# Layer norms' normalising, a convolution tap and copies moved from VectorE to ScalarE in a fused decoder layer

## The chip, the cores and the metric

One core of a Trainium2 chip runs the whole kernel. The metric is device time of one execution in microseconds, median of the runs made.

## The reference

The input x has 16 sequences of 128 positions and 256 features. Three sub-layers are added to it, each behind a layer norm without gain:

```python
x = x + mamba(layernorm(x))             # in_proj, 4-tap convolution, silu, scan of 16 states, gate, out_proj
x = x + mlstm(layernorm(x), ctx, ctx)   # 4 heads of 64; gates from concat(q, k, v) @ kernel
x = x + ffn(layernorm(x))               # 6 attention nodes in a graph, then a layer norm with gain and offset
```

Where it matters here: the convolution is `sum over k of w[k] * x[t + k - 1] + b`. The gates take `concat([q, k, v]) @ kernel` with k = v = ctx. The mLSTM's head is divided by `normalizer + 1e-6` and then normalised over its 64 features, `(h - mean) * rsqrt(var + 1e-6) * scale`. The silu is computed with a tanh, so weights of the convolution are halved ahead (`convh`).

## The kernel before

The batch is cut into 8 groups of 2 sequences (256 columns, or 128 partitions by 2 by 256 features). Each group goes through three streams of steps, and all engines walk one list, `ORDER`, in which the steps of neighbouring groups are interleaved: each engine runs, of each step, what it has to do in it, in order. `ORDER` is sorted by numbers written out by hand for each step (`A_AT`, `U_AT`, `X_AT`, `P_AT`), counted in steps of the feed-forward net of the group that runs at that time. The streams are:

- **A**, eleven steps (`mamba_in`): norm 1 (step 0), its transposes (1), four input projections (2 to 5) through one PSUM bank `MA`, the convolution on VectorE (4), silu and gate, the projections of step sizes; then **U**, 32 *units* (`unit`): on ScalarE two exponentials for the decay (`dec`, L753, two buffers), on VectorE a product to feed (L972), a scan (L979) and a weighing (L990), on TensorE the sums over states (L487), and after eight units a `gather`.
- **X**, the mLSTM (`mlstm`, `head_scores`, `head_values`, `head_norm`, `mlstm_out`): out projection and norm 2 (`ml` 1), gates, four heads, their norm, norm 3 (`out` 0) and its transposes (`out` 1), which give node -1 of the net.
- **F**, the net (`queries`, `keys`, `values`, `node_max`, `node_score`, `node_attend`, `node_edge`, `node_out`) with 6 nodes one after the other, and `ffn_out` with norm 4, gain, offset, the residual and the store.
- **P**, the preparation of the net's weights, only at the start.

While F of group g runs, the units of group g+1 end, its X runs and the units of group g+2 begin. F of the last group runs alone.

A layer norm (`layer_norm` on VectorE) is BATCH_NORM_STATS (L911), aggregation (L915), the addition of epsilon (L917), then a wait for ScalarE (`rstd_of`: a logarithm L678 and an exponential L679) and two TENSOR_SCALAR (L920), one per sequence:

```python
for b in range(GB):
    last = v.tensor_scalar(dst[:, b, :], src(b), mean_var[:, b, 0:1], inv[:, b:b + 1],
                           ALU.subtract, ALU.mult)
```

The convolution reads `hs_pad`, which ScalarE copies from `MA` (L705); its first tap is a TENSOR_SCALAR (L934), the three others are L941. `head_values` copies each head out of PSUM (L1049). `head_norm` divides all heads by their denominators (L1062), takes the mean (L1063), subtracts it (L1065), squares (L1066), sums (L1067) and scales (L1070, L1073). The gate product (L516) multiplies three times two blocks of `wgate`.

## Time and profile before

| | us |
|---|---|
| median of 3 runs | 1309.74 (1309.69 to 1315.06) |
| the profiled execution | 1308.01 |
| its span, first to last instruction | 1306.2 |
| VectorE (DVE) busy | 1053.6 |
| TensorE (PE) busy | 1098.0 |
| ScalarE (ACT) busy | 720.6 |

The rows come from the profiled execution. A row of the waits gives the time for which an engine stood idle and the engine, tile and line that released it; a row of the groups gives busy time (overlap counted once) and the mean duration of one; a row of the timeline gives start, duration, engine, line, and in brackets the idle time before it. PE is TensorE's matmul, PEld its weight load. Busy time of stretches is cut where the net of a group ends (L655).

### The profile page before, as it was taken

How to read it: one execution, taken by the hardware profiler on the slowest of the kernel's cores; microseconds unless marked ns; L12 is line 12 of the kernel's file. 1: busy time of each engine (PE TensorE's matmuls, PEld its weight loads, DVE VectorE, ACT ScalarE, POOL GpSimd, SP SyncE). 2: the span in 40 equal slices, each digit the busy share in tenths (PEclk: the TensorE clock that was granted, in tenths of full speed). 3: DMA queues.
4: the chain of work that ended last, by engine and by line, in shares of the span. 5: the costliest groups of instructions: out<-in, count | busy, mean ns of one | idle time of the engine just before them, and what ended most of it. 6: DMA issues, size and time to landing. Idle time of an engine off the chain costs nothing. (4 is left out here: it accounts for less than half of the span.)

```text
span 1306.2 us, 27811 instructions
## 1 busy us (share of the span) xinstructions
PE 1098.0 (84%) x11504; PEld 822.0 (63%) x11504; DVE 1053.6 (81%) x1683; ACT 720.6 (55%) x1692; POOL 2.9 (0%) x10
## 2 busy tenths in 40 slices
PE   3845668988999899989988998899888988897886
PEld 2723445766676667666666666666666666676665
DVE  2289887799999999999999999999999889725112
ACT  1434532576657665776567556755576646444332
POOL 0000000000000000000000000000000000000000
PEclk9767775999999999999999999999999989999998
DMA  6440343004100410030112211030104000000000
GB/s 190 122 178 32 107 153 113 33 3 130 41 26 33 132 42 25 34 105 28 50 49 62 71 50 49 16 117 33 58 3 130 33 25 34 2 1 10 2 1 9
DMA packets 53710, 76.14 MB, mean 58 GB/s; under 512 B 15376, under 2 KB 38672, under 8 KB 53456
## 3 DMA queue, kind: packets, MB, share of 16 engines
q1 hardware_dynamic: 53584, 74.37, 17.9%
q8 instruction: 90, 1.47, 0.5%
q14 instruction: 36, 0.29, 0.1%
HBM read 63.60 MB, written 10.75 MB: 57 GB/s over the span
## 5 line engine op out<-in xcount | busy, mean ns | idle before, releaser
L979 DVE TENSOR_TENSOR_SCAN unit_buf<-dec,unit_buf 128x512 f32<-128x512 f32 x256 | 311.9, 1218 | 11.7 <-ACT dec L753 11.0
L753 ACT ACTIVATE dec<-dts,a_neg 128x254 f32<-128x254 f32 x512 | 225.6, 499 | 42.5 <-DVE unit_buf L979 37.3
L972 DVE TENSOR_TENSOR unit_buf<-dtus,bs 128x512 f32<-128x512 f32 x256 | 175.0, 686 | 6.3 <-DMA dtus<-dt_rows 2.5
L990 DVE TENSOR_TENSOR unit_buf<-unit_buf,cs 128x512 f32<-128x512 f32 x256 | 175.3, 685 | 0.5
L1087 DVE TENSOR_REDUCE mx<-heads 128x16 f32<-128x2048 f32 x48 | 109.2, 2276 | 50.1 <-PE heads L602 50.0
L487 PE MATMUL ps<-unit_buf,fold 128*32 128x256 f32 x1024 | 89.0, 420 | 52.4 <-DVE unit_buf L990 52.3
L825 ACT ACTIVATE pr<-heads 128x512 f32<-128x512 f32 x192 | 99.1, 603 | 49.0 <-PE heads L617 49.0
L571 PE MATMUL ps<-node,wq_f 128*128 128x256 f32 x384 | 93.6, 387 | 7.8 <-ACT node L840 7.8
L640 PE MATMUL heads<-node,we_f 128*128 128x256 f32 x384 | 94.7, 389 | 0.0
L647 PE MATMUL heads<-aT,wo_f 128*128 128x256 f32 x384 | 93.7, 387 | 0.9 <-DVE aT L1096 0.9
L581 PE MATMUL heads<-wv_f,node 128*128 128x256 f32 x384 | 91.8, 382 | 0.0
L571 PEld LDWEIGHTS ps<-node,wq_f 128*128 128x128 f32 x384 | 70.6, 190 | 27.8 <-ACT node L840 11.1
L647 PEld LDWEIGHTS heads<-aT,wo_f 128*128 128x128 f32 x384 | 69.6, 190 | 18.7 <-issue 5.8
L640 PEld LDWEIGHTS heads<-node,we_f 128*128 128x128 f32 x384 | 69.5, 190 | 17.7 <-issue 9.9
L556 PE MATMUL ps<-node,wk_f 128*128 128x256 f32 x320 | 80.0, 393 | 0.0
L581 PEld LDWEIGHTS heads<-wv_f,node 128*128 128x128 f32 x384 | 71.8, 190 | 12.1 <-issue 2.9
L815 ACT ACTIVATE kT<-ps,fb 128x256 f32<-128x256 f32 x80 | 33.4, 469 | 79.4 <-PE ps L556 79.4
L487 PEld LDWEIGHTS ps<-unit_buf,fold 128*32 128x32 f32 x1024 | 21.9, 111 | 86.8 <-DVE unit_buf L990 54.2
L602 PE MATMUL heads<-kT,qT 32*128 32x128 f32 x1536 | 57.2, 285 | 20.8 <-issue 11.7
L452 PE MATMUL ps<-th,win 128*128 128x256 f32 x256 | 71.5, 427 | 3.6 <-ACT hs_pad L705 1.5
L602 PEld LDWEIGHTS heads<-kT,qT 32*128 32x128 f32 x1536 | 48.9, 188 | 37.1 <-issue 36.3
L840 ACT ACTIVATE node<-heads,fb 128x256 f32<-128x256 f32 x96 | 40.1, 468 | 56.1 <-PE heads L647 56.0
(178 smaller groups left out, 1777.8 us busy)
## 6 DMA issues: line engine op xcount, KB each, us to landing
dts<-dt_rows SPq DMA_DIRECT2D x32, 512.0 KB, 3.8
dtus<-dt_rows SPq DMA_DIRECT2D x32, 512.0 KB, 5.2
node<-in_w_edgeT SPq DMA_DIRECT2D x18, 256.0 KB, 3.6
dt_rows<-dt SPq DMA_DIRECT2D x32, 128.0 KB, 2.4
dt_rows<-th SPq DMA_DIRECT2D x32, 128.0 KB, 2.5
bs<-bc_rows SPq DMA_DIRECT2D x32, 128.0 KB, 4.6
cs<-bc_rows SPq DMA_DIRECT2D x32, 128.0 KB, 4.3
xin<-in_x SPq DMA_DIRECT2D x8, 256.0 KB, 6.2
```

The costliest lines, as they stand in the source:

```text
L487: last = mm(MY[r0:r0 + SD, 0:T], fold[:], prd[(i * UNITS + k) % PRDS][:, a, :], start=(q == 0), stop=(q == NGRP - 1), tile_position=(0, r0))
L571: last = mm(FA[:, a * T:(a + 1) * T], wq_f[c][:, k, a * P:(a + 1) * P], src[:, k, :], start=(a == 0 and k == 0), stop=(k == HC - 1), skip_ ...
L581: last = mm(X3[:, b * H:(b + 1) * H], node[SLOT[GRAPH[c]["v"]]][:, k, b * L:(b + 1) * L], wv_f[c][:, k, :], start=(k == 0), stop=(k == HC ...
L602: last = mm(heads[:, h, to], qT[at], kT[c % 2][at], start=True, stop=True, tile_position=(FD * h, 0))
L640: mm(X1[:, a * T:(a + 1) * T], we_f[c][:, k, a * P:(a + 1) * P], src[:, k, :], start=(a == 0 and k == 0), stop=False, skip_group_check=True)
L647: last = mm(X1[:, a * T:(a + 1) * T], wo_f[c][:, k, a * P:(a + 1) * P], aT[:, k, :], start=False, stop=(k == HC - 1), skip_group_check=True)
L753: last = fn(dec[k % 2][:, a, :, 1:L], dts[c % 2][:, blk, :].rearrange("p (b t) -> p b t", b=GB)[:, :, 1:L], ACT.Exp, scale=a_neg[:, c, blk ...
L825: fn(pr[s][:], heads[:, :, s * L:(s + 1) * L], ACT.Exp, scale=FD ** -0.5).then_inc(sig["prob"], 1)
L972: v.tensor_tensor(inf[k % 2][:], dtus[c % 2][:, 2 * pair:2 * pair + 2, :], bs[:, q:q + 1, :].broadcast_to([P, 2, T]), ALU.mult).then_inc(s ...
L979: v.tensor_tensor_scan(hst[k % 2][:].rearrange("p a b -> p (a b)"), dec[k % 2][:].rearrange("p a b t -> p (a b t)"), inf[k % 2][:].rearran ...
L990: v.tensor_tensor(prd[(i * UNITS + k) % PRDS][:], hst[k % 2][:], cs[:, q:q + 1, :].broadcast_to([P, 2, T]), ALU.mult).then_inc(sig["outflo ...
L1087: v.tensor_reduce(mx[:].rearrange("p (h s) -> p h s", h=HPC)[:, :, 0:STEPS], heads[:].rearrange("p h (s k) -> p h s k", s=STEPS), AX.X, AL ...
```

## The change

Normalising moves to ScalarE in all four norms: `layer_norm` on VectorE ends with a negation of the mean and the addition of epsilon, and `normalise` on ScalarE multiplies the negated mean by the root and applies both as scale and bias of an Identity. VectorE waits before it overwrites mean and variance the next time, and in norm 4 for the rows. The tap with k = 1 of the convolution, which needs no shift, is taken by ScalarE straight from PSUM with the bias; VectorE does the taps 0, 2 and 3. `head_values` moves to ScalarE. In `head_norm` the heads are not divided by the denominator any more: mean and variance are taken of the undivided heads, the variance is multiplied twice by the reciprocal denominator before epsilon is added, the root once after; the square is done by ScalarE, between two waits. The two blocks of gate kernel rows for k and v are added once, and the gate product has four blocks instead of six. All four tables of numbers are others.

```diff
-    ln_var1=1, ln_rstd1=1, hvar=1, hrstd=1,
+    ln_var1=1, ln_rstd1=1, hcentre=1, hsquare=1, hvar=1, hrstd=1,
...
-A_AT = [-90, -86, -76, -69, -62, -58, -57, -52, -44, -43, -42]
+A_AT = [-99, -84, -76, -71, -69, -58, -57, -52, -50, -47, -40]
...
-X_AT = [18, 38, 43, 44, 47, 48, 49, 51, 53, 54, 55, 57, 58, 60, 63, 65]
+X_AT = [4, 38, 43, 44, 48, 49, 50, 52, 54, 55, 56, 57, 58, 59, 63, 65]
...
 # TensorE, mlstm step 3
-                    for k in range(3 * HC):
+                    for k in range(2 * HC):
...
 # ScalarE
+            def normalise(chain, n, i, src, mean_var, inv, dst):
+                rstd_of(chain, f"ln_var{n}", f"ln_rstd{n}", i, inv[:])
+                after(act, f"ln_rstd{n}", i, 1)
+                for b in range(GB):
+                    m = chain.mark(fn(mean_var[:, b, 0:1], mean_var[:, b, 0:1], ACT.Copy, scale=inv[:, b:b + 1]))
+                chain.wait(m)
+                for b in range(GB):
+                    last = fn(dst[:, b, :], src(b), ACT.Identity, scale=inv[:, b:b + 1], bias=mean_var[:, b, 0:1])
+                return last
...
+                    after(act, "y_ready", i - 2, IC)
+                    for a in range(2):
+                        c = 2 * j + a
+                        last = fn(u[p][:, c, :], MA[:, a * T:(a + 1) * T], ACT.Identity,
+                                  scale=convh[:, 5 + c * 4:6 + c * 4], bias=convh[:, c:c + 1])
                     last.then_inc(sig["inproj_read"], 1)
...
+            def head_values(i, h):
+                after(act, "h_ps", i, h + 1)
+                fn(hrow[:, :, h, :], MB[:, 0:GB * XP].rearrange("p (b d) -> p b d", b=GB), ACT.Copy
+                   ).then_inc(sig["h_read"], 1)
+
             def head_norm(i, _):
+                after(act, "hcentre", i, 1)
+                fn(hsq, hn, ACT.Square).then_inc(sig["hsquare"], 1)
                 rstd_of(m_chain, "hvar", "hrstd", i, hva[:])
...
 # VectorE, layer_norm
+                v.tensor_scalar(mean_var[:, :, 0], mean_var[:, :, 0], -1.0, None, ALU.mult)
                 v.tensor_scalar(inv[:], mean_var[:, :, 1], eps, None, ALU.add).then_inc(sig[f"ln_var{n}"], 1)
-                after(dve, f"ln_rstd{n}", i, 1)
-                for b in range(GB):
-                    last = v.tensor_scalar(dst[:, b, :], src(b), mean_var[:, b, 0:1], inv[:, b:b + 1],
-                                           ALU.subtract, ALU.mult)
-                return last
...
 # VectorE, convolution
-                    for k in range(1, 4):
+                    marks = [0] * IC
+                    for k in (0, 2, 3):
...
 # VectorE, mlstm step 1, group 0
+                        v.tensor_tensor(wgate[:, HC:2 * HC, :], wgate[:, HC:2 * HC, :], wgate[:, 2 * HC:3 * HC, :],
+                                        ALU.add).then_inc(sig["gate_sum"], 1)
...
 # VectorE, head_norm
-                m_chain.link(v.tensor_tensor(hn, hn, den[:].unsqueeze(2).broadcast_to(wide), ALU.mult))
...
-                m_chain.link(v.tensor_tensor(hsq, hn, hn, ALU.mult))
+                v.tensor_tensor(hn, hn, hmu[:].unsqueeze(2).broadcast_to(wide), ALU.subtract).then_inc(sig["hcentre"], 1)
+                after(dve, "hsquare", i, 1)
                 m_chain.link(v.tensor_reduce(hva[:], hsq, AX.X, ALU.add))
-                v.tensor_scalar(hva[:], hva[:], 1.0 / XD, HEAD_EPS, ALU.mult, ALU.add).then_inc(sig["hvar"], 1)
+                m_chain.link(v.scalar_tensor_tensor(hva[:], hva[:], 1.0 / XD, den[:], ALU.mult, ALU.mult))
+                m_chain.link(v.tensor_tensor(hva[:], hva[:], den[:], ALU.mult))
+                v.tensor_scalar(hva[:], hva[:], HEAD_EPS, None, ALU.add).then_inc(sig["hvar"], 1)
                 after(dve, "hrstd", i, 1)
+                m_chain.link(v.tensor_tensor(hva[:], hva[:], den[:], ALU.mult))
...
 # VectorE, ffn_out
+                after(dve, "rows_read", i - 1, 1)
+                layer_norm(i, f_chain, 4, lambda b: X1[:, b * H:(b + 1) * H], fmv, fbn, frstd, OUT_EPS)
                 after(dve, "rows_read", i, 1)
```

Three places of the order, in a full turn (the net of group 3). Line numbers are those of each kernel. First VectorE at the heads' norm, before: `mx` is the maximum of node 5, L1049 the copy of the last head.

```order
L1087 TENSOR_REDUCE mx<-heads 128x4x4
L1049 COPY hrow<-ps 128x2x65
L1058 SCALAR_TENSOR_TENSOR den<-hrow 128x8
L1059 TENSOR_TENSOR den<-den,em 128x8
L1060 TENSOR_SCALAR den<-den 128x8
L1061 RECIPROCAL den<-den 128x8
L1062 TENSOR_TENSOR hrow<-hrow,den 128x8x64
L1063 TENSOR_REDUCE hmu<-hrow 128x8
L1064 TENSOR_SCALAR hmu<-hmu 128x8
L1065 TENSOR_TENSOR hrow<-hrow,hmu 128x8x64
L1066 TENSOR_TENSOR ml_buf<-hrow 128x512
L1067 TENSOR_REDUCE hva<-ml_buf 128x8
```

And now:

```order
L1111 TENSOR_REDUCE mx<-heads 128x4x4
L993 TENSOR_TENSOR unit_buf<-dtus,bs 128x512
L1011 TENSOR_TENSOR unit_buf<-unit_buf,cs 128x512
L1000 SCALAR_TENSOR_TENSOR unit_buf<-dec,unit_buf 128x512
L1079 SCALAR_TENSOR_TENSOR den<-hrow 128x8
L1080 TENSOR_TENSOR den<-den,em 128x8
L1081 TENSOR_SCALAR den<-den 128x8
L1082 RECIPROCAL den<-den 128x8
L1083 TENSOR_REDUCE hmu<-hrow 128x8
L1084 TENSOR_SCALAR hmu<-hmu 128x8
L1085 TENSOR_TENSOR hrow<-hrow,hmu 128x8x64
L1087 TENSOR_REDUCE hva<-ml_buf 128x8
```

A unit (L993, L1011, L1000) stands between the maximum and the norm, the copy is gone, and so are the product with `den` and the square; the sum over the squares (L1087) follows the subtraction.

Then VectorE at norm 3 (`mbn`, `mmv`) and norm 4 (`fbn`, `fmv`), before:

```order
L911 BN_STATS mbn<-xr 128x6 x2
L915 BN_AGGR mmv<-mbn 128x2 x2
L917 TENSOR_SCALAR mrstd<-mmv 128x2
L920 TENSOR_SCALAR hrow<-xr,mmv,mrstd 128x256 x2
L972 TENSOR_TENSOR unit_buf<-dtus,bs 128x512
L990 TENSOR_TENSOR unit_buf<-unit_buf,cs 128x512
L979 SCALAR_TENSOR_TENSOR unit_buf<-dec,unit_buf 128x512
L911 BN_STATS fbn<-heads 128x6 x2
L915 BN_AGGR fmv<-fbn 128x2 x2
L917 TENSOR_SCALAR frstd<-fmv 128x2
L920 TENSOR_SCALAR aT<-heads,fmv,frstd 128x256 x2
```

And now, where L943 is the negation and L962 the convolution:

```order
L937 BN_STATS mbn<-xr 128x6 x2
L941 BN_AGGR mmv<-mbn 128x2 x2
L943 TENSOR_SCALAR mmv<-mmv 128x2
L944 TENSOR_SCALAR mrstd<-mmv 128x2
L962 SCALAR_TENSOR_TENSOR u<-hs_pad,convh,u 128x256 x12
L937 BN_STATS fbn<-heads 128x6 x2
L941 BN_AGGR fmv<-fbn 128x2 x2
L943 TENSOR_SCALAR fmv<-fmv 128x2
L944 TENSOR_SCALAR frstd<-fmv 128x2
L1128 TENSOR_TENSOR aT<-aT,rowv 128x512
L1129 TENSOR_TENSOR aT<-aT,rowv 128x512
L1130 TENSOR_TENSOR aT<-aT,xr 128x512
```

The normalising is gone from both, the unit that stood between them comes after norm 4, and the convolution, which stood behind the next maximum, stands between them.

Last ScalarE at the same place, before: the last two divisions of node 5 (L834, L835), norm 3 (`mrstd`), a decay, the reads of node 5 (`node<-heads`) and of node -1 (`node<-ps`).

```order
L834 ACTIVATE aT<-heads 128x256
L835 ACTIVATE aT<-aT 128x256
L678 ACTIVATE mrstd<-mrstd 128x2
L679 ACTIVATE mrstd<-mrstd 128x2
L753 ACTIVATE dec<-dts,a_neg 128x2x127 x2
L840 ACTIVATE node<-heads,fb 128x256 x2
L705 ACTIVATE hs_pad<-ps 128x2x128 x2
L799 ACTIVATE node<-ps 128x512
```

And now, with L680 to L691 the norm:

```order
L861 ACTIVATE aT<-aT 128x256
L860 ACTIVATE aT<-heads 128x256
L861 ACTIVATE aT<-aT 128x256
L719 ACTIVATE hs_pad<-ps 128x2x128 x2
L724 ACTIVATE u<-ps,convh 128x256 x2
L680 ACTIVATE mrstd<-mrstd 128x2
L681 ACTIVATE mrstd<-mrstd 128x2
L688 ACTIVATE mmv<-mmv,mrstd 128x1 x2
L691 ACTIVATE hrow<-xr,mmv,mrstd 128x256 x2
L866 ACTIVATE node<-heads,fb 128x256 x2
L731 ACTIVATE gate<-ps 128x512
L825 ACTIVATE node<-ps 128x512
```

The normalising stands ahead of node 5's reads, the decay went behind, and a gate's read (L731) stands ahead of the copy of node -1. At norm 2 the table puts one unit (2) right behind the norm on VectorE, where before the divisions of node 3 came first; at norm 1 a weighing, the maximum of node 3 and a gather stand between norm and next scan.

## Rows read from the trace of the kernel before

**Rows 1.** The page: span, and busy time of each engine with its share.

```profile
span 1306.2 us, 27811 instructions
...
PE 1098.0 (84%) x11504; PEld 822.0 (63%) x11504; DVE 1053.6 (81%) x1683; ACT 720.6 (55%) x1692; POOL 2.9 (0%) x10
```

**Rows 2.** Busy time by stretch; columns: PE, PEld, DVE, ACT, POOL, clock, DMA share, GB/s.

```profile
376.10:513.20 137.10, 124.13 (x1397) 92.61 (x1397) 129.66 (x205) 87.68 (x210) 0.00 (x0) 1.00 0.18 55
...
925.40:1063.20 137.80, 122.65 (x1376) 91.61 (x1376) 128.12 (x198) 86.33 (x204) 0.00 (x0) 0.98 0.17 53
1063.20:1190.10 126.90, 109.74 (x1295) 83.50 (x1296) 85.72 (x134) 63.35 (x158) 0.00 (x0) 0.99 0.04 14
1190.10:1297.90 107.80, 89.39 (x1116) 73.36 (x1114) 23.10 (x28) 43.01 (x99) 0.00 (x0) 0.95 0.01 4
```

**Rows 3.** Waits of TensorE, 376.1 to 1063.2 us; us in total, times, longest.

```profile
PE ps L609 <- DVE mx L1087: 10.5, 15, 1.5
PE ps L609 <- ACT kT L815: 8.9, 10, 1.4
PE heads L602 <- issue: 7.3, 10, 0.7
PE ps L487 <- DVE unit_buf L990: 7.2, 19, 0.5
PE ps L629 <- ACT pr L825: 6.9, 10, 0.7
```

**Rows 4.** Waits of VectorE in the same stretch.

```profile
DVE hrow L920 <- ACT mrstd L679: 5.1, 10, 0.5
DVE hrow L1049 <- PE ps L544: 3.8, 5, 0.8
...
DVE hrow L1070 <- ACT hva L679: 2.6, 5, 0.5
DVE aT L920 <- ACT frstd L679: 2.5, 5, 0.5
...
DVE th L920 <- ACT rstd L679: 2.0, 4, 0.5
```

**Rows 5.** Timeline at norm 3 of group 4: start, duration, engine, line.

```profile
786.12 0.17 DVE L917 TENSOR_SCALAR mrstd<-mmv 128x2 f32<-128x2 f32 x1
...
786.67 0.89 ACT L753 ACTIVATE dec<-dts,a_neg 128x254 f32<-128x254 f32 x2
786.79 0.74 DVE L920 TENSOR_SCALAR hrow<-xr,mmv,mrstd 128x256 f32<-128x256 f32 x2 [0.51 <-ACT mrstd L679]
```

**Rows 6.** Groups of VectorE, 376.1 to 1063.2 us; busy us, mean ns, idle before.

```profile
L920 DVE TENSOR_SCALAR hrow<-xr,mmv,mrstd 128x256 f32<-128x256 f32 x20 | 7.4, 410 | 5.1 <-ACT mrstd L679 5.1
L934 DVE TENSOR_SCALAR u<-hs_pad,convh 128x256 f32<-128x256 f32 x20 | 6.9, 410 | 0.0
...
L1049 DVE COPY hrow<-ps 128x130 f32<-128x130 f32 x20 | 5.7, 282 | 3.8 <-PE ps L544 3.8
L920 DVE TENSOR_SCALAR aT<-heads,fmv,frstd 128x256 f32<-128x256 f32 x10 | 5.0, 539 | 2.5 <-ACT frstd L679 2.5
...
L1066 DVE TENSOR_TENSOR ml_buf<-hrow 128x512 f32<-128x512 f32 x5 | 3.5, 692 | 0.2
```

**Rows 7.** Groups of ScalarE, whole span.

```profile
L805 ACT ACTIVATE qT<-ps,fb 128x256 f32<-128x256 f32 x96 | 40.2, 470 | 32.7 <-PE ps L571 32.6
...
L835 ACT ACTIVATE aT<-aT 128x256 f32<-128x256 f32 x96 | 40.0, 417 | 3.0
...
L767 ACT ACTIVATE ml_buf<-ps 128x512 f32<-128x512 f32 x8 | 4.8, 597 | 1.5 <-PE ps L435 1.0
```

**Rows 8.** Timeline of TensorE: the context's part of a gate product.

```profile
603.64 1.89 PE L516 MATMUL ps<-ctxT,wgate 128*36 128x256 f32 x8
```

**Rows 9.** Waits of TensorE, whole span: the wait for the first weights.

```profile
PE ps L435 <- DMA win<-in_w_in: 18.2, 1, 18.2
```

**Rows 10.** Timeline of VectorE at the start: a TENSOR_SCALAR of 512 columns.

```profile
37.04 0.48 DVE L891 TENSOR_SCALAR we_f<-node,vec 128x512 f32<-128x512 f32 x1
```

More of the change, by code:

```diff
@@ L928, in mamba_in @@
                     after(dve, "x_loaded", i, 16)
[L929 to L930 removed]
+                    after(dve, "ln1_rows", i - 1, 1)
+                    layer_norm(i, a_chain, 1, lambda b: xin[:, b, :], mv, bn, rstd, LN_EPS)
                 if step == 4:
                     after(dve, "inproj_read", i, 2)
[L934 to L937 removed]
+                    marks = [0] * IC
+                    for k in (0, 2, 3):
                         for c in range(IC):
[L939 removed]
+                            if k:
+                                a_chain.wait(marks[c])
                             uc = u[p][:, c, :].rearrange("p (b t) -> p b t", b=GB)
```

56 lines of the change are left out of this document (25 added, 31 removed).

## The prediction

> **What bounds the kernel now.** I read the page first: VectorE is busy 1053.6 us and TensorE 1098.0 us of a span of 1306.2 us, ScalarE only 720.6 [rows 1]. Shares over the whole span say little here, so the second view is busy time by stretch, cut at the transposes that end each group's feed-forward net (the steps F, one *turn* from one such end to the next). Five turns, from 376.1 to 1063.2 us, are alike: 137.4 us each (687.1 / 5), VectorE busy some 129.7, TensorE some 124.1, ScalarE 87.6; the granted clock of TensorE is 0.98 to 1.00, so its level of 2.4 GHz nearly throughout [rows 2]. So VectorE is full to 94% and TensorE to 90%: VectorE sets the pace, and TensorE stands close behind with 13.3 us of idle per turn. In the next stretch (126.9 us) VectorE is busy 85.7 us only, since the state-space units run out in it, and in the last one (107.8 us, F alone) 23.1 [rows 2]: what VectorE is spared there buys nothing by itself.
>
> The third view, waits of the five turns, says whom the two wait for. TensorE's largest waits are for VectorE's maximum (10.5 us), ScalarE's keys (8.9), VectorE's weighing (7.2), ScalarE's probabilities (6.9) and issue (7.3) [rows 3]: both engines that feed it hold it up, in about equal parts. VectorE's are short: 5.1 us for the roots of the middle layer norms, 2.5 and 2.0 for those of the last and the first, 2.6 for the heads' root, 3.8 for the heads' values [rows 4]. These it all pays with idle time, since it is in order and nothing lies behind the wait.
>
> **The change, part by part**, in VectorE's time per turn.
>
> *Layer norms 1 to 3.* Today VectorE writes the variance, waits for ScalarE's logarithm and exponential, and normalises two halves: in the timeline the variance's add starts at 786.12 us and takes 0.17, the normalising starts at 786.79 after 0.51 us of idle and takes 0.74 [rows 5]. The change takes wait and normalising away (1.25 us) and adds a negation like the add, 0.17 us and a little gap: 1.05 saved, three times, 3.1 us. The two halves are 410 ns each [rows 6]. For the reader behind it it gets later: ScalarE now does 0.45 us for the root, two products of one column (each like a 0.20 us root step) and two Identities of 256 columns. Nearest row: an Identity with one per-partition operand, 470 ns, against 417 with none [rows 7]; so I take 520 ns for one with two, about 0.95 us for a pair that overlaps a little. That is 1.8 us from variance to rows, where it was 1.24: 0.55 later.
>
> *Layer norm 4.* Here VectorE needs the rows at once for gain and offset, and waits for them. It gives up 0.51 + 1.0 us (two of 539 ns that overlap) [rows 6] and pays 0.2 + 1.8: a loss of 0.5 us per turn.
>
> *First tap.* Four TENSOR_SCALAR, 6.9 us in the five turns [rows 6], so 1.4 per turn, leave VectorE; its later taps are twelve fused multiply-adds before and after. ScalarE gets four Identities from PSUM, 1.7 to 1.9 us, and the bank that the next input projection needs comes free 0.9 us later, twice per turn. I cost that at nothing, since the projections stand far apart in the order; without that cover it is 1.8 us of TensorE.
>
> *Heads' values.* Four copies, 5.7 us in the five turns [rows 6] and 3.8 of waiting [rows 4]: 1.1 + 0.8 = 1.9 us per turn leave VectorE. ScalarE takes them at about 0.28 each.
>
> *Heads' norm.* The division by the denominator (0.69 us, same form as the square) goes, the square (0.69) moves [rows 6]; three operations on eight columns come (0.2 each), and VectorE now waits for the square, which on ScalarE is about 0.6 us (a 512-column copy is 597 ns) [rows 7]. 1.4 against 1.25: 0.1 saved, if ScalarE is free. The order tells that it stands behind the four probability exponentials of node 5, but that one more unit of VectorE's (2.6 us) is now ahead of the norm, so they should be over.
>
> *Gates.* The context's part of the gate product is 1.89 us [rows 8]; half of it goes, 0.95 us of TensorE per turn, against one addition once.
>
> Sum per turn on VectorE: 3.1 - 0.5 + 1.4 + 1.9 + 0.1 = **6.0 us**. ScalarE gets some 5.4 (norms) + 1.8 + 1.1 + 0.6 = 8.9 us more, 87.6 to about 96.5. Over the run: norm 1 and tap (2.4) count for groups 1 to 7, norms 2 and 3, copies and heads (4.1) for groups 0 to 6, norm 4 (-0.5) for seven. 17 + 28.5 - 3.5 = 42. Group 7's heads lie where VectorE has slack: nothing. At the start ScalarE's longer chain (0.55 us in the norm) hides behind the weights, for which TensorE waits 18.2 us [rows 9]; the longer reads before the convolution (1.7 us) and the tap saved (1.4) cancel. The preparation of weights moves against the first units too; no row prices that, I take nothing, and a few us either way lie in the range. The last norm costs 0.6 at the very end. **41 us** if VectorE alone decides.
>
> It does not alone. A turn of 131.4 us leaves TensorE, with 123.2 us of work, 8.2 us idle where it has 13.3 now. The waits that VectorE causes should shrink, those for ScalarE should not: its queue is longer by 8.9 us, and in the new order the head norm and norm 3 stand ahead of node 5's divisions and reads. There I count 0.65 us by which node 5 is read later (0.2 for the negation and 1.35 for the longer norm, less the unit's exponential, 0.9 us [rows 5], that moved behind), 0.6 for the gate's read that now stands ahead of the copy for the next net's first keys (512 columns [rows 7]), and 0.5 at the heads' norm. So I give back 1.7 us per turn, 12 in seven: **29 us** are left. 1308.0 us, the profiled execution's own time (1.8 us above its span), less 29 is 1279; the median of the three runs is 1.7 us above that execution, so **1280** us.
>
> *A rule against the tap and the norms.* What the rows show: the moved single-source operations of 256 columns are 410 ns each, 344 from start to start [rows 6], and one of 512 columns takes 0.48 us [rows 10], less than the 692 ns of a two-source one of that size [rows 6]. The Trainium skill (VectorE: DVE Perf Modes, "The perf-mode tier table") says that fp32 tensor_scalar between SBUF tiles runs at twice the rate of two-source operations, so exactly the cheap work would leave VectorE and the dear work stay; the 512-column row agrees. By its figure (1227 ns for 2048 columns, so some 290 for 256, an estimate) the saving would be 0.6 us per turn smaller.
>
> The Trainium skill (ScalarE: Activation LUTs, "What ACT_TABLE_LOAD costs") gives 93 ns for each per-partition operand of an activation; with it the pairs would cost ScalarE some 0.5 us per turn more than I take. No row before shows an activation with two.
>
> **Rivals.** (a) *VectorE alone decides*: TensorE's waits shrink with VectorE's load, all 41 us arrive, 1268. For it: 17.7 us of the five turns' waits on TensorE come from VectorE [rows 3]. Against: 15.8 come from ScalarE in two rows alone.
> (b) *TensorE and the net's chain take over*: ScalarE's added reads stand ahead of the net's, TensorE keeps its idle time but for the gates, and a turn falls by 1 to 2 us. Seven turns: 7 to 14 us, 1296 to 1303.
> (c) *Slower*: ScalarE's queue. If all 8.9 us stand ahead of keys, queries, node reads and decays, TensorE's idle grows by 8.9 us per turn, and a turn gets 8.9 - 6.0 = 3 us longer, 21 in seven: 1330. It decides from 6 us of new waiting per turn on. The places are the three where VectorE goes straight on to a unit: it reaches the scan after a feed and a weighing, 1.3 us, while the decay waits for 1.8 us of norm and then takes 0.9. Against it: ScalarE would still be idle a quarter of the turn, and behind norm 1 and norm 3 the new order puts a maximum and the twelve taps on VectorE before the next scan; only behind norm 2 does a unit follow at once.
> (d) *No change that can be measured*, within 0.5% (6.5 us, about what a measurement of this kernel can tell from none): new waits for the square, the rows and the decays eat 5 of the 6 us.
> That a table of functions would be reloaded for the square or the identities can be put aside: both orders have the same 17 loads.
>
> **Chances.** Forecast, a gain of 17 to 38 us: 0.57. (a) 0.12. (b) 0.15. (d) 0.08. (c) 0.08. Faster by over 0.5% is the first three, 0.84; same 0.08; slower 0.08. The range leaves out the far part of (a), where the new order would beat its own sum, and (c) with most of (d): 1264 to 1302.
>
> **What would show it.** Right: turns of about 133 us, VectorE busy some 123.5 in each, TensorE 123; no more waits of VectorE for the roots of norms 1 to 3, some 1.8 us per turn for the rows of norm 4 and some 0.6 for the square; ScalarE some 96 us; the last stretch (107.8 us) within 1 us of what it was. Wrong: decays as VectorE's largest releaser, or turns above 136 us with TensorE's waits for ScalarE's keys, nodes and probabilities grown by as much as VectorE saved.

## The result, and the profile after

The change makes the kernel **slower: 1349.16 us** (median of 4 runs, 1347.19 to 1351.6) against 1310.11 of the kernel before in the same comparison (1309.69 to 1315.06), ratio 1.0296 with a 95% interval of 1.0278 to 1.0313. The profiled execution took 1348.6 us.

The page answers to [rows 1]. VectorE lost what was forecast (1053.6 to 1011.0 us) and ScalarE gained what was forecast (720.6 to 793.9), and the span grew by 40.5 us. In the chain of work that ended last, TensorE has more than half:

```profile
span 1346.7 us, 27889 instructions
...
PE 1111.1 (83%) x11472; PEld 830.9 (62%) x11472; DVE 1011.0 (75%) x1596; ACT 793.9 (59%) x1892; POOL 2.9 (0%) x10
...
PE 53%; DVE 20%; ACT 17%; issue 8%; SPq 1%; DMA 1%; DVEq 0%; ACTq 0%
```

The same stretches as in [rows 2], cut where a group's net ends (length, then busy time of PE, PEld, DVE, ACT, POOL, granted clock, DMA share, GB/s):

```profile
388.40:532.00 143.60, 126.96 (x1393) 94.14 (x1393) 124.55 (x194) 96.79 (x235) 0.00 (x0) 0.98 0.18 53
...
953.60:1094.70 141.10, 120.35 (x1364) 89.44 (x1365) 120.47 (x180) 91.46 (x219) 0.00 (x0) 0.97 0.17 52
1094.70:1229.50 134.80, 116.35 (x1293) 88.41 (x1291) 80.28 (x126) 69.56 (x176) 0.00 (x0) 0.93 0.04 13
1229.50:1337.80 108.30, 89.52 (x1114) 72.59 (x1114) 22.18 (x27) 44.22 (x103) 0.00 (x0) 0.95 0.01 4
```

The start takes 388.4 us instead of 376.1 (+12.3), the five turns 706.3 instead of 687.1 (+19.2, so 141.3 for 137.4), the sixth 134.8 for 126.9 (+7.9), the last one, F alone, 108.3 for 107.8. In the first turn VectorE works 124.55 us where it worked 129.66, and is idle 19.1 us instead of 7.4. What it waits for (us in total, times, longest; the five turns, as [rows 4]):

```profile
DVE unit_buf L1000 <- ACT dec L772: 18.0, 22, 1.7
DVE u L1018 <- PE ps L487: 13.4, 6, 4.8
DVE mx L1111 <- PE heads L604: 12.6, 16, 1.5
DVE aT L1128 <- ACT aT L691: 10.3, 5, 2.1
...
DVE hva L1087 <- ACT ml_buf L816: 3.5, 5, 0.7
```

None of [rows 4]'s waits for roots of norms 1 to 3 is left. In their place stand the decays (2.9 us before), the sums over states for the gather (1.4 before), the net's scores for a maximum (0.6 before), the rows of norm 4 and the square. TensorE's waits in the same stretch of five turns, as [rows 3]:

```profile
PE ps L487 <- DVE unit_buf L1011: 14.9, 14, 1.6
PE ps L611 <- ACT kT L841: 10.8, 15, 1.0
PE ps L631 <- ACT pr L851: 10.4, 15, 0.7
PE ps L474 <- ACT dt L754: 8.3, 5, 1.7
PE heads L604 <- ACT vrow L836: 8.2, 5, 1.6
```

It waits less for VectorE's maxima (10.5 us in [rows 3], 1.3 now), and more for VectorE's weighing and for most of ScalarE's results (step sizes 4.9 us before, values none, though 7.3 us of "issue" at the same line are gone, node reads for the queries 5.4 before and 8.1 now; its waits for the queries stay at 3.3). The timeline shows how a decay gets late, behind norm 2 of a middle turn (start, duration, engine, line; in brackets the idle time before):

```profile
755.37 0.16 DVE L944 TENSOR_SCALAR mrstd<-mmv 128x2 f32<-128x2 f32 x1
755.43 0.69 DVE L993 TENSOR_TENSOR unit_buf<-dtus,bs 128x512 f32<-128x512 f32 x1
755.56 0.20 ACT L680 ACTIVATE mrstd<-mrstd 128x2 f32<-128x2 f32 x1 [3.81 <-DVE mrstd L944]
...
756.03 0.48 ACT L688 ACTIVATE mmv<-mmv,mrstd 128x1 f32<-128x1 f32 x2
756.55 1.09 ACT L691 ACTIVATE hrow<-xr,mmv,mrstd 128x256 f32<-128x256 f32 x2
...
757.54 0.89 ACT L772 ACTIVATE dec<-dts,a_neg 128x254 f32<-128x254 f32 x2
...
758.46 1.23 DVE L1000 TENSOR_TENSOR_SCAN unit_buf<-dec,unit_buf 128x512 f32<-128x512 f32 x1 [1.74 <-ACT dec L772]
```

ScalarE, in order, stands 3.81 us at the norm for VectorE's variance, then works 2.1 us on it, and only then takes the decay; VectorE arrives at the scan after 1.3 us of unit work and waits 1.74. Behind the decay the divisions of node 3 wait too. The longest instructions for which the prediction had no row (mean ns of one, whole span):

```profile
L691 ACT ACTIVATE hrow<-xr,mmv,mrstd 128x256 f32<-128x256 f32 x32 | 17.5, 593 | 0.5
L724 ACT ACTIVATE u<-ps,convh 128x256 f32<-128x256 f32 x32 | 16.4, 572 | 0.0
...
L816 ACT ACTIVATE ml_buf<-hrow 128x512 f32<-128x512 f32 x8 | 5.1, 632 | 4.6 <-DVE hrow L1085 4.6
```

Three things could be behind the 40 us: the new order (the tables), the added work on ScalarE, or the clock; and whether VectorE's saving is worth anything is a question by itself.

### The profile page after: what moved, and what is told of

Read it like the earlier page. It is cut to its first block, busy times and chain, and to the rows that moved or that the text cites. A ratio compares the mean times of both kernels' runs of the same rounds, so it can differ in the third digit from the quotient of the medians.

```text
span 1346.7 us, 27889 instructions
## 1 busy us (share of the span) xinstructions
PE 1111.1 (83%) x11472; PEld 830.9 (62%) x11472; DVE 1011.0 (75%) x1596; ACT 793.9 (59%) x1892; POOL 2.9 (0%) x10
## 4 chain that ended last, share of the span: by engine, by line
PE 53%; DVE 20%; ACT 17%; issue 8%; SPq 1%; DMA 1%; DVEq 0%; ACTq 0%
DVE unit_buf L1000 6%; PE ps L573 5%; PE heads L583 5%; PE heads L649 4%; PE heads L642 4%; PE ps L452 4%; PE heads L604 4%; PE ps L558 4%; PE ps L487 3%; DVE unit_buf L1011 3%; ACT pr L851 3%; ACT dec L772 3%; PE heads L419 2%; PE ps L506 2%; PE heads L614 2%
## 5 line engine op out<-in xcount | busy, mean ns | idle before, releaser
L1000 DVE TENSOR_TENSOR_SCAN unit_buf<-dec,unit_buf 128x512 f32<-128x512 f32 x256 | 312.3, 1220 | 37.3 <-ACT dec L772 37.1
L993 DVE TENSOR_TENSOR unit_buf<-dtus,bs 128x512 f32<-128x512 f32 x256 | 175.1, 687 | 11.9 <-DMA dtus<-dt_rows 7.1
L1011 DVE TENSOR_TENSOR unit_buf<-unit_buf,cs 128x512 f32<-128x512 f32 x256 | 175.4, 685 | 0.5 <-DVE fb L929 0.2
L851 ACT ACTIVATE pr<-heads 128x512 f32<-128x512 f32 x192 | 99.1, 604 | 41.4 <-PE heads L619 41.4
L642 PE MATMUL heads<-node,we_f 128*128 128x256 f32 x384 | 103.2, 416 | 0.0
L573 PE MATMUL ps<-node,wq_f 128*128 128x256 f32 x384 | 92.9, 385 | 10.9 <-ACT node L866 10.9
L583 PE MATMUL heads<-wv_f,node 128*128 128x256 f32 x384 | 92.2, 383 | 0.0
L642 PEld LDWEIGHTS heads<-node,we_f 128*128 128x128 f32 x384 | 75.4, 204 | 21.5 <-issue 11.6
L573 PEld LDWEIGHTS ps<-node,wq_f 128*128 128x128 f32 x384 | 71.5, 191 | 25.7 <-ACT node L866 14.1
L649 PEld LDWEIGHTS heads<-aT,wo_f 128*128 128x128 f32 x384 | 70.5, 191 | 25.0 <-DVE aT L1120 10.5
L583 PEld LDWEIGHTS heads<-wv_f,node 128*128 128x128 f32 x384 | 72.0, 190 | 12.8 <-issue 2.9
```

Source lines behind the costliest of these rows:

```text
L573: last = mm(FA[:, a * T:(a + 1) * T], wq_f[c][:, k, a * P:(a + 1) * P], src[:, k, :], start=(a == 0 and k == 0), stop=(k == HC - 1), skip_ ...
L583: last = mm(X3[:, b * H:(b + 1) * H], node[SLOT[GRAPH[c]["v"]]][:, k, b * L:(b + 1) * L], wv_f[c][:, k, :], start=(k == 0), stop=(k == HC ...
L642: mm(X1[:, a * T:(a + 1) * T], we_f[c][:, k, a * P:(a + 1) * P], src[:, k, :], start=(a == 0 and k == 0), stop=False, skip_group_check=True)
L649: last = mm(X1[:, a * T:(a + 1) * T], wo_f[c][:, k, a * P:(a + 1) * P], aT[:, k, :], start=False, stop=(k == HC - 1), skip_group_check=True)
L851: fn(pr[s][:], heads[:, :, s * L:(s + 1) * L], ACT.Exp, scale=FD ** -0.5).then_inc(sig["prob"], 1)
L993: v.tensor_tensor(inf[k % 2][:], dtus[c % 2][:, 2 * pair:2 * pair + 2, :], bs[:, q:q + 1, :].broadcast_to([P, 2, T]), ALU.mult).then_inc(s ...
```

## The experiments

All times are medians against the kernel before on the same chip, whose medians were 1308.8 to 1310.6 us; a loss "by its ratio" is that share of 1310 us. The table takes the four turns between the first and the fifth end of a net; TensorE's idle time is the turn less its busy time. These columns come from one profiled execution of each kernel. Executions of one kernel lie up to 14 us apart (e9 from 1297.9 to 1312.1), so some tenths of a microsecond between two turns decide nothing. e5, e9, e13, e14, e17 and e18 leave results out and only measure what work costs.

| kernel | median us | ratio (95%) | turn | DVE, ACT busy | PE busy | PE idle | clock |
|---|---|---|---|---|---|---|---|
| before | 1310 | | 137.3 | 129.7, 87.7 | 124.5 | 12.8 | 1.00 |
| the change | 1349.2 | 1.030 (1.028 to 1.031) | 141.3 | 124.5, 96.6 | 124.9 | 16.4 | 0.99 |
| e1 change, old tables | 1389.5 | 1.062 (1.057 to 1.066) | 151.6 | 124.5, 96.8 | 132.8 | 18.8 | 0.93 |
| e2 new tables alone | 1442.5 | 1.102 (1.100 to 1.105) | 156.7 | 130.5, 87.5 | 133.2 | 23.5 | 0.93 |
| e3 undivided heads, gates | 1304.5 | 0.996 (0.994 to 0.998) | 136.8 | 129.4, 87.7 | 123.5 | 13.3 | 1.00 |
| e4 norms 1 to 3 | 1350.4 | 1.031 (1.028 to 1.033) | 143.3 | 128.1, 92.2 | 126.1 | 17.3 | 0.99 |
| e5 change, short Identities | 1344.7 | 1.028 (1.025 to 1.031) | 142.0 | 124.4, 95.1 | 126.2 | 15.8 | 0.98 |
| e6 norm 2 | 1322.9 | 1.010 (1.007 to 1.014) | 139.0 | 128.9, 89.2 | 125.4 | 13.6 | 0.99 |
| e7 norm 3 | 1325.4 | 1.013 (1.009 to 1.016) | 139.7 | 129.3, 89.4 | 125.1 | 14.6 | 0.99 |
| e8 first tap | 1317.9 | 1.008 (1.005 to 1.010) | 138.3 | 128.6, 89.5 | 124.8 | 13.5 | 0.99 |
| e9 less on VectorE | 1307.3 | 0.996 (0.993 to 0.999) | 136.4 | 127.0, 87.8 | 123.6 | 12.8 | 1.00 |
| e10 more on ScalarE | 1353.6 | 1.032 (1.031 to 1.034) | 144.3 | 130.1, 92.9 | 126.9 | 17.4 | 0.98 |
| e11 change, norm 4 and square back | 1345.0 | 1.027 (1.025 to 1.029) | 142.0 | 126.0, 95.0 | 126.1 | 15.9 | 0.98 |
| e12 heads' values | 1309.8 | 1.000 (0.999 to 1.001) | 137.4 | 129.0, 88.5 | 124.5 | 12.9 | 1.00 |
| e13 less on ScalarE | 1307.1 | 0.999 (0.997 to 1.001) | 136.7 | 129.3, 83.0 | 124.1 | 12.6 | 1.00 |
| e14 less on TensorE | 1321.5 | 1.010 (1.008 to 1.012) | 139.1 | 129.6, 87.9 | 123.9 | 15.2 | 0.98 |
| e15 more on VectorE | 1324.3 | 1.012 (1.010 to 1.014) | 139.2 | 131.7, 87.6 | 125.1 | 14.1 | 0.99 |
| e16 e3, net's values on VectorE | 1371.3 | 1.048 (1.046 to 1.050) | 146.8 | 133.2, 84.4 | 129.1 | 17.7 | 0.95 |
| e17 e9 and e13 | 1295.7 | 0.987 (0.984 to 0.991) | 135.6 | 126.9, 83.0 | 124.2 | 11.4 | 0.99 |
| e18 e9, e13 and e14 | 1298.7 | 0.990 (0.986 to 0.994) | 135.5 | 126.9, 83.1 | 121.8 | 13.7 | 0.99 |

Of the ranges stated ahead of the runs, e1, e2, e4, e10, e14, e15 and e16 met none (e1, e2, e4, e10 and e16 came out slower than every one of them, e14 too; e15 between two), and e12 fell just between two. e5 and e11 fell where the shorter work on ScalarE was expected to bring little.

### Tables or work: e1, e2

e1 is the change with the numbers of before, e2 the kernel before with the numbers of the change:

```diff
-A_AT = [-99, -84, -76, -71, -69, -58, -57, -52, -50, -47, -40]
+A_AT = [-90, -86, -76, -69, -62, -58, -57, -52, -44, -43, -42]
```

(so e1; `U_AT`, `X_AT` and `P_AT` likewise; e2 the other way round.)

> The whole change, but with the four tables of numbers of the kernel before. Theory 1, the new order: VectorE's work fell by 42 us as summed, and the loss (VectorE idle 16.8 us per turn instead of 7.7) comes from where the new tables put steps (gathers right behind their sums, maxima right behind keys, decays behind the norm). Then this run is at or below the kernel before, 1280 to 1310 us. Theory 2, ScalarE's queue: whatever the tables, the 8.9 us per turn that went to ScalarE stand ahead of decays and of the net's reads. Then this run is as slow as the change or slower, 1340 to 1375 us, with VectorE's wait for the decay (18.0 us in five turns in the change, 2.9 before) as large or larger.

> The kernel before with the four new tables and nothing else of the change. Theory 1: slower than before by 20 to 40 us, 1330 to 1350. Theory 2: within 10 us of before, 1300 to 1320.

Neither is anywhere near the kernel before: by their ratios the work without its tables costs 81 us, the tables without their work 134, and the change 39. The new order is thus no culprit that could be taken out. It belongs to the change and gives 42 of e1's 81 us back. In both, two things add up (table): TensorE's idle time grows by 6 and 11 us per turn, and its busy time by over 8 although it does the same or less work, since the granted clock is 0.93 over the four turns, so for part of them at 1.2 instead of 2.4 GHz:

```profile
389.60:996.00 606.40, 531.06 (x5568) 394.46 (x5568) 498.18 (x773) 387.30 (x937) 0.00 (x0) 0.93 0.16 50
```

The kernel before has 498.06 us for 5584 matmuls in its four turns. e2's waits of VectorE in its four turns, where ScalarE does nothing new:

```profile
DVE unit_buf L993 <- ACT dec L764: 24.7, 17, 2.8
...
DVE mx L1103 <- PE heads L602: 12.0, 14, 1.7
DVE u L1011 <- PE ps L487: 11.5, 5, 3.3
```

The gather's and the maxima's waits of the change (9.8 and 9.2 us in its four turns) are of the same size as here. e1, without the tables, has them too (7.3 and 13.0), so which of the two makes them in the change stays open.

### Part by part: e3, e4, e6, e7, e8, e12

Each is the kernel before with one part, old tables. e3 has the two parts that give ScalarE nothing:

```diff
-                    for k in range(3 * HC):
+                    for k in range(2 * HC):
...
-                m_chain.link(v.tensor_tensor(hn, hn, den[:].unsqueeze(2).broadcast_to(wide), ALU.mult))
```

(with the small products on `hva`, and the square still on VectorE.)

> The kernel before, old tables, with only the two parts that move nothing to ScalarE: heads not divided (VectorE loses a product of 0.69 us and gains three small operations of 0.2, so about 0.1 us per turn) and the gates' kernel rows added up once (0.95 us of TensorE per turn). Both theories: 1 to 7 us below before, 1303 to 1309.

5.5 us faster by its ratio, the whole interval below 1: the **version that beats both kernels**. e4 moves the normalising to ScalarE for norms 1 to 3, e6 and e7 for one each (here e6; norm 1 was not run alone):

```diff
-                    rstd_of(m_chain, "ln_var2", "ln_rstd2", i, mrstd[:])
+                    normalise(m_chain, 2, i, lambda b: xr[i % 2][:, b, :], mmv, mrstd, mrow).then_inc(sig["ln2_rows"], 1)
...
-                    layer_norm(i, m_chain, 2, lambda b: xi[:, b, :], mmv, mbn, mrstd, LN_EPS, mrow).then_inc(sig["ln2_rows"], 1)
+                    layer_norm(i, m_chain, 2, lambda b: xi[:, b, :], mmv, mbn, mrstd, LN_EPS)
```

> The kernel before, old tables, with the normalising of norms 1 to 3 on ScalarE and nothing else. If VectorE's sum decides (3.1 us per turn): 1288 to 1295 us. Theory 2: ScalarE's queue grows by about 4 us per turn at three places, two of them with a unit right behind the norm in the old order; the scan then waits for its decay about 1.5 us at each, and the reads of node 5 come later: 1305 to 1325 us, with more than 5 us of new waits for decays in the five turns.

> The kernel before, old tables, with norm 2 alone normalised on ScalarE. In the old order the divisions of node 3 stand right behind it on ScalarE, and their products on VectorE: it waits there instead (3.3 us per turn in the run with norms 1 to 3). If the three norms of that run, 40 us, cost alike: 1320 to 1326. If the divisions behind norm 2 are the cause: 1325 to 1345.

> The kernel before, old tables, with norm 3 alone normalised on ScalarE. A unit stands right behind it on VectorE, and the reads of node 5 behind it on ScalarE. Equal shares: 1320 to 1326. If the divisions behind norm 2 are the cause: 1308 to 1318, with about 1.5 us per turn of new wait for the decay against 1.05 saved.

e4 alone costs 40 us by its ratio, as much as the whole change. VectorE is spared only 1.6 us of busy time per turn in it besides its waits, ScalarE gets 4.6, and the turn is 6.0 longer. Norm 2 costs 13.6 us by its ratio and norm 3 16.5. Where VectorE pays is another place each time, first e6, then e7 (four turns):

```profile
DVE aT L1112 <- ACT aT L846: 12.6, 8, 2.9
```

```profile
DVE unit_buf L993 <- ACT dec L764: 10.5, 13, 1.7
DVE mx L1103 <- PE heads L602: 6.0, 8, 2.1
```

In e6 it is the divisions of node 3 behind the norm (1.2 us before), in e7 the decays (2.2 us before) and then the net's next maximum (0.6 before).

e8 takes the tap, e12 the heads' values:

```diff
+                        last = fn(u[p][:, c, :], MA[:, a * T:(a + 1) * T], ACT.Identity,
```

```diff
+                fn(hrow[:, :, h, :], MB[:, 0:GB * XP].rearrange("p (b d) -> p b d", b=GB), ACT.Copy
```

> The kernel before, old tables, with the first tap alone on ScalarE. VectorE loses 1.4 us per turn. If VectorE's sum decides: 1298 to 1304. Theory 2: ScalarE's 1.8 us per turn stand behind projections, ahead of a decay or of the heads' exponentials: 1308 to 1320.

> The kernel before, old tables, with the copies of the heads' values alone on ScalarE. VectorE loses 1.1 us of work and 0.8 us of waits per turn. If its sum decides: 1295 to 1302. Theory 2: the copies wait in ScalarE's queue behind decays, so the next head's scores come later: 1310 to 1322.

The tap costs 10 us by its ratio and the heads' values nothing, though they take 0.7 us per turn of busy time from VectorE, and the waits (1.9 together in the prediction). Each of the parts run here that hands work over costs time or gives nothing; only e3's, which removes work, gains.

### Length of the added work: e5, e10, e11

e5 leaves the Identities of all four norms at one column, e11 takes norm 4 and the square back to VectorE, both with the change's tables:

```diff
-                    last = fn(dst[:, b, :], src(b), ACT.Identity, scale=inv[:, b:b + 1], bias=mean_var[:, b, 0:1])
+                    last = fn(dst[:, b, 0:1], src(b)[:, 0:1], ACT.Identity, scale=inv[:, b:b + 1], bias=mean_var[:, b, 0:1])
```

```diff
-                fn(hsq, hn, ACT.Square).then_inc(sig["hsquare"], 1)
...
+                m_chain.link(v.tensor_tensor(hsq, hn, hn, ALU.mult))
```

> The change with its own tables, but each of the two Identities of every norm on ScalarE writes one column of 256 (the normalised rows are left out; all waits, signals and other operations stay). ScalarE then has some 1.5 us less per turn for each pair, in the four norms about 1.7 (0.21 us of streaming for each Identity, eight of them). Theory 2 (the length of what ScalarE does ahead of decays and reads): the wait behind norm 2 (1.74 us) and the wait for the rows of norm 4 (2.07 us) shrink by 0.4 us each and the turn falls by 1 to 3 us, 1325 to 1342. Theory 3 (the place of ScalarE's wait in its queue, not the length of the work): 1343 to 1350, as the change.

> The change with its own tables, but norm 4's normalising and the heads' square back on VectorE. VectorE works 1.7 us more per turn (1.0 + 0.7) and waits 2.1 - 0.5 at norm 4 and 0.7 at the square less. By the sum of VectorE: 0.6 us per turn less, 1342 to 1348. Theory 2: ScalarE's queue is 2.3 us per turn shorter at the turn from one net to the next, where node 5 and the next keys are read: 1325 to 1342.

They gain 2 and 4 us of the 39 by their ratios; e5's interval overlaps the change's widely and e11's by a little, and their turns are no shorter. In e5 ScalarE has 1.5 us less per turn and the waits for decays and for norm 4 are shorter (12.8 and 6.6 us in the four turns, for 15.2 and 8.3), but VectorE's wait for the sums before a gather grows from 9.8 to 16.0. So in the change neither the Identities' length nor VectorE's new wait for norm 4 (2.07 us per turn) is the cause by itself. e10 is the other way round, the kernel before with four idle Identities of 64 columns behind the root of norms 1 to 3, nothing taken from VectorE:

```diff
+                if done_sig in ("ln_rstd1", "ln_rstd2", "ln_rstd3"):
+                    for _k in range(4):
+                        chain.link(fn(spare[:], cst[:, 0:L // 2], ACT.Identity, scale=ones[:, 0:1], bias=ones[:, 1:2]))
```

> The kernel before, old tables, with four Identities of 64 columns (one after the other, some 0.3 us each) put on ScalarE behind the root of norms 1 to 3, after its signal, so that VectorE's own normalising is not delayed: about 1.2 us three times per turn, 3.7 us. Theory 2 (length of ScalarE's queue): most of the loss of norms 1 to 3 on ScalarE (40 us) appears here too, 1330 to 1350. If it is the delay of the rows and of the waiting structure instead: 1310 to 1320.

42 us of loss, the decisive run: three times 1.84 us on ScalarE (timeline at norm 2) make the turn 7.0 us longer.

```profile
471.15 0.20 ACT L680 ACTIVATE mrstd<-mrstd 128x2 f32<-128x2 f32 x1
471.26 1.84 ACT L683 ACTIVATE spare<-cst,ones 128x64 bf16<-128x64 f32 x4
473.14 0.38 ACT L838 ACTIVATE aT<-ps 128x256 f32<-128x256 f32 x1
```

Waits of TensorE in its four turns; queries and node reads are the net's chain. Before, the first stood at 2.6 us in 4 waits and the second at none:

```profile
PE heads L603 <- ACT qT L809: 10.1, 8, 2.1
PE heads L656 <- ACT node L844: 7.9, 4, 2.0
```

TensorE's idle time grows by 4.6 us per turn, about the added 5.2, and its busy time by 2.4 at a clock of 0.98. That is the size of e4's loss, made without touching a norm. It shows that work added to ScalarE at these places is enough by itself, in the old order; with the new tables no run adds or removes as much.

### What is each engine worth: e9, e13, e14, e15, e17, e18, e16

These ask the question that the prediction answered from busy shares. e9 cuts VectorE's normalising, tap, division and scaling to a column:

```diff
-                    last = v.tensor_scalar(dst[:, b, :], src(b), mean_var[:, b, 0:1], inv[:, b:b + 1],
+                    last = v.tensor_scalar(dst[:, b, 0:1], src(b)[:, 0:1], mean_var[:, b, 0:1], inv[:, b:b + 1],
```

e13 cuts ScalarE's copies of the net's values and the second step of its divisions:

```diff
-                fn(vrow[:].rearrange("p a b -> p (a b)"), X3, ACT.Copy).then_inc(sig["v_ready"], 1)
+                fn(vrow[:, 0, 0:1], X3[:, 0:1], ACT.Copy).then_inc(sig["v_ready"], 1)
...
-                    fn(dinv[:, m, :], dinv[:, m, :], ACT.Exp, scale=-1.0).then_inc(sig["den_inv"], 1)
+                    fn(dinv[:, m, 0:1], dinv[:, m, 0:1], ACT.Exp, scale=-1.0).then_inc(sig["den_inv"], 1)
```

> The kernel before, old tables, with VectorE's work taken away and nothing given to ScalarE: the eight normalising operations write one column of 256, the four of the first tap one column, the division of the heads and their scale one column of 64 (those results are left out). VectorE is spared about 0.45 us at each of norms 1 to 3, 0.6 at norm 4, 1.1 at the tap, 1.0 at the heads: 4.1 us per turn. If VectorE's work sets the pace as the prediction had it: turns of 133.3 us, in all 1278 to 1284 us. Theory 4, TensorE and the net's chain stand too close behind, so that VectorE's savings turn into waits whatever ScalarE does: turns of 135.5 to 137.4 us, 1295 to 1310.

> The kernel before, old tables, with ScalarE's work taken away: the copy of the net's values writes one column of 512 (0.42 us less, six per turn) and the exponential of the twelve reciprocals one column of 256 (0.21 us less); those results are left out. ScalarE is spared 5 us per turn. Theory 5, ScalarE stands in the chain from TensorE to TensorE, so that the turn follows its work in both directions (3.7 us more cost 6.9 us per turn): 4 to 9 us less per turn, 1250 to 1285 us. Theory 6, a balance: the hand-made order has every engine just in time, so that more on any engine costs and less on one alone gives little: 0 to 2 us less per turn, 1296 to 1310.

Both four turns, first e9, then e13:

```profile
376.70:922.50 545.80, 494.22 (x5587) 371.59 (x5586) 507.95 (x818) 351.23 (x837) 0.00 (x0) 1.00 0.17 55
```

```profile
380.60:927.20 546.60, 496.40 (x5584) 370.46 (x5584) 517.28 (x817) 331.82 (x837) 0.00 (x0) 1.00 0.18 55
```

VectorE with 2.7 us less work per turn gives a turn 0.9 us shorter (and the run 5 us by its ratio); ScalarE with 4.7 less gives 0.6. If VectorE had set the pace, the first would have been 2.7. Over the whole run e13's gain, 1.4 us, can't be told from none, and e9's lies between 1 and 9 us of the 19 that 2.7 us make in seven turns: its fifth turn, at a granted clock of 0.93, took 142.9 us where that of before took 137.8 at 0.98.

e14 leaves out all columns but one in half of the sums over states on TensorE; e18 does this with e9's and e13's cuts, e17 has the two cuts alone:

```diff
-                        last = mm(MY[r0:r0 + SD, 0:T], fold[:], prd[(i * UNITS + k) % PRDS][:, a, :],
+                        w = T if q in (0, NGRP - 1) else 1
+                        last = mm(MY[r0:r0 + SD, 0:w], fold[:], prd[(i * UNITS + k) % PRDS][:, a, 0:w],
```

> The kernel before, old tables, with TensorE's work taken away: of the sixteen sums over states per turn eight multiply one column instead of 256 (their share of y is left out), some 0.3 us each, 2.5 us per turn, and TensorE's queue is shorter by as much. Theory 4, TensorE is the pace: 2 to 3 us less per turn, 1288 to 1296. Theory 6: 0 to 1 us less, 1302 to 1310.

> The kernel before, old tables, with the work of e9 and that of e13 taken away together (VectorE 4.1 us less per turn, ScalarE 5.0; the same results are left out). If each was only held up by the other: turns of 133 us or less, 1280 us or below. If TensorE and the net's chain set the pace: the two small gains add up at most, 1.5 us per turn, turns of 135.5 to 136.5, 1295 to 1304, with TensorE busy 91% of a turn and idle about 12 us as before.

> As e17, and the eight sums over states of one column as in e14. If TensorE's work sets the pace: 2.5 us per turn below e17, some 18 to 20 us in all. If its granted clock falls when it has less to do, as in e14 (0.98 in the turns against 1.00, and 1.8 us per turn slower): at or above e17.

e17's turn is 1.7 us shorter, about the sum of 0.9 and 0.6: TensorE keeps its 124 us of work and has 11.4 idle. The run gains 17 us by its ratio, though, against 5 and 1 of the two cuts alone: outside the four turns, in the start (371.3 us for 376.7 and 380.6) and in the fifth turn (136.7 for 142.9 and 138.1), the two together did better than either. How much of that is the clock wasn't separated. e14 is slower by 1.0%. Its sums over states, the row of its four turns, took 41.4 us there before (394 ns each):

```profile
L488 PE MATMUL ps<-unit_buf,fold 128*32 128x1 f32 (+1 forms) x512 | 28.3, 285 | 7.1 <-DVE unit_buf L991 7.1
```

That is 3.3 us per turn less, yet TensorE's busy time falls by 0.6 only, and its idle time grows by 2.4. Turn by turn, the granted clock tells the slow ones from the fast one (the third and the fourth):

```profile
657.30:797.20 139.90, 124.77 (x1396) 94.91 (x1396) 129.41 (x205) 87.73 (x210) 0.00 (x0) 0.98 0.17 54
797.20:934.00 136.80, 121.45 (x1396) 92.39 (x1396) 129.61 (x205) 87.76 (x210) 0.00 (x0) 1.00 0.17 54
```

The first three take 139.8 to 140.0 us at 0.98, the fourth 136.8 at 1.00, with the same work: some 3 us for one spell of about 7 us at 1.2 GHz (483.8 to 490.7 in the first turn). Shortly ahead of it, from 479.5 to 482.5, TensorE was busy 2.18 us of 3.0, against 2.57 at that place before. In the fourth turn it was 2.18 us as well, and the clock stayed; why it falls in three turns of four isn't shown. The fourth is 0.3 us shorter than the 137.1 of a turn of before at 1.00 [rows 2], so that is what the cut is worth there, and the lower clock takes ten times that back. The same comparison can be made for the others, turns at 1.00 against 137.1 to 137.3: the change's second and third take 140.3 and 140.2, so 3 of its 4 us per turn are there without the clock; e4 has one of 142.2, e10 one of 142.6, e15 139.0, e9 136.3 to 136.6, e17 135.3 and 135.6. Added to e17, the cut gives the mean turn nothing (135.5 for 135.6; 134.9 and 135.1 at 1.00), although TensorE has 2.4 us less to do, and the run takes 3 us more, within what the two intervals allow to be zero. So TensorE's work isn't what sets the pace either.

e15 adds four idle products on VectorE behind norms 1 to 3, e16 gives VectorE the copy of the net's values on top of e3:

```diff
+                    for _k in range(4):
+                        chain.link(v.tensor_scalar(spare[:], cst[:, 0:L // 2], 1.0, None, ALU.mult))
```

```diff
+            def values(i, c):
+                after(dve, "v_ps", i, c + 1)
+                v.tensor_copy(vrow[:].rearrange("p a b -> p (a b)"), X3).then_inc(sig["v_ready"], 1)
```

> The kernel before, old tables, with four operations of 64 columns (one after the other, some 0.25 us each) put on VectorE behind norms 1 to 3, after its signal that the rows are there: the mirror of the run with more on ScalarE, 3 us per turn. If VectorE has no slack, as its 94% busy say: 3 us per turn, 1331 to 1336. If its work is hidden behind TensorE and ScalarE, as the run with less of it says: below 1 us per turn, 1310 to 1318. If it is amplified as ScalarE's was: above 1340.

> The kernel before, old tables, heads not divided, gates added up once (1304.5 us), and the copy of the net's values out of PSUM moved from ScalarE to VectorE: the opposite direction to the change, 3.6 us per turn. Theory 5: 1275 to 1295. Theory 6, or VectorE without slack: 1310 to 1335, since it waits in its queue for TensorE's product.

e15's 2.0 us more busy make the turn 1.9 longer. e16 is the change's direction reversed: ScalarE is spared 3.2 us per turn, and the run takes 67 us more than e3's (1371.3 against 1304.5). The copy waits in VectorE's queue behind units, and TensorE for it (the first row, 5.9 us before, has no releaser that the profile names):

```profile
PE heads L604 <- issue: 20.9, 8, 3.0
PE heads L604 <- DVE vrow L1107: 9.6, 4, 2.5
```

So the kernel before is **balanced on both sides**: 2 us more on VectorE are paid in full, 5 us more on ScalarE at the norms one and a third times, while 2.7 or 4.7 us less bring a third or an eighth of it in these turns.

## Why the prediction was wrong

It forecast 1280 us, at the most 1302 by its range. The sum of VectorE's work was nearly right, its value was not.

- **"VectorE sets the pace, and TensorE stands close behind"** is the step that failed. It rested on 94% against 90% busy [rows 2]. e9 puts the price on it: a microsecond taken from VectorE's busy time is worth a third of one in these turns (0.9 of 2.7), while one added costs all of it (e15). What holds a turn at 135 us or more is not one engine's work: 7.5 us less on VectorE and ScalarE together gave 1.7, and 2.4 less on TensorE on top of that gave nothing (e17, e18). That it is the net's chain through all three is the likely reading, not shown by a run. The 6.0 us were therefore worth about 2 (0.9 / 2.7 of them, an estimate), 13 in seven turns instead of 41.
- **The give-back of 1.7 us per turn** was the second mis-sized term. It counted three places where a read gets later. e10 shows the price of ScalarE at these places without any order or saving in play: 7.0 us for 5.2. Here the prediction looked only at who reads next, and not at everything that stands behind it in ScalarE's queue. In the change's own order the size of this term stays open: of its turns at the full clock, 3 us longer than before, the new places and the added work have shares that no run separates. Nor had it a term for TensorE's clock, which fell from 0.99 to 0.93 in the sixth stretch (109.7 to 116.4 us busy for as many matmuls, 6.6 of its 7.9 us more).
- **The terms of VectorE's sum** nearly held. Expected was 123.5 us of busy time, measured 124.5 (the tap gives 1.1 for 1.4 in e8, the heads' copies 0.7 for 1.1 in e12), with the waits for the roots gone as said. Norm 4's wait was to be 1.8 us and is 2.07; the square 0.6 and is 0.7; the gates 0.95 us of TensorE and, over 8 groups, L516 and L518 went from 25.2 to 18.4 us, so 0.85.
- **ScalarE's 8.9 us** came out exactly (87.7 to 96.6), in part by luck: three norms are 4.6 us in e4 and not 4.05, the heads' copies 0.8 in e12 and not 1.1. The pair of Identities was taken as 0.95 us and is 1.02 to 1.09. The Trainium skill (ScalarE: Activation LUTs, "What ACT_TABLE_LOAD costs") gives 93 ns for each per-partition operand; two such operands make 593 ns here, against 417 with none [rows 7], so 88 each. By this figure, as an estimate, a pair would have been some 0.15 us longer than the prediction took it, which doesn't change the sign of the result.
- **The tap at nothing**: the cover that it named, projections that "stand far apart", held in the turns: none of e8's four turns has a wait of a projection for the tap (the start has 4.0 us of them). But nothing was counted for the rest of ScalarE's queue: in the four turns TensorE waits 5.2 us for node -1 instead of 1.5, and 6.5 instead of 4.3 for the node reads ahead of the queries. e8 gives 10 us of loss with 1.1 us per turn taken from VectorE; of the 13.6 in its profiled execution 7.9 are in the start (384.0 us), 4.0 in the four turns.
- **The cancelling at the start** (1.7 against 1.4 us) was not borne out: the first stretch is 12.3 us longer. In it, from 70 us on, the scans wait 17.3 us for decays instead of 2.4, and TensorE is busy 247.9 us instead of 238.1 at a granted clock of 0.80 instead of 0.83. How much of this the new places of the units make and how much ScalarE, was not separated; with the old places e4 has 385.5, e10 386.5 and e1 389.6, so added work on ScalarE lengthens the start without new places, and e2, with new places alone, has 408.1.
- **Rival (c) was the right mechanism**, even its place: behind norm 2, where a unit follows at once, it worked out a wait of 1.4 us (1.8 + 0.9 against 1.3), and 1.74 was measured. It gave 3 us per turn and 1330 us in all; 4.0 and 1349 came, with 3.6 us more idle time of TensorE per turn where it had 8.9. Its chance of 0.08 rested on "it decides from 6 us of new waiting", which took VectorE's 6.0 at full value. At a third of it, 2 us of waiting would have been enough, and the forecast's own 1.7 nearly that.
- **What would show it wrong** did in the main: decays as VectorE's largest releaser, turns above 136 us. The waits of TensorE for ScalarE's keys, nodes and probabilities grew by 8 us in the five turns, though, not by the 28 that VectorE's busy time fell.

The sum of the single parts (e4 40, e8 10, e12 0, e3 -5.5 us; norm 4 and the square not run alone) is near 44, e1 with all of them 81. The missing 37 are norm 4, the square, or what the parts do to each other, with the clock at 0.93 in the one and 0.99 to 1.00 in the others; which of these is not shown (in the new order norm 4 and the square together are worth 4, e11). From e1 to the change TensorE's busy time per turn falls by 7.9 us of the 10.3 by which the turn gets shorter, so most of what the tables recover there goes with the clock. Whether tables exist that make the change as fast as e3 wasn't tried.
